# Another way to the global maximum, clips on GpSimd, and other orders at both ends of a Mamba kernel

## The reference

```
x, z = split(h @ W_in.T)                        # 256 channels each
x    = silu(conv4(x) + conv_b)                  # causal, per channel
dt, B, C = split(x @ Wx.T)                      # 64, 16, 16
dt   = softplus(dt @ Wdt.T + bdt)
s[t] = exp(dt*A) * s[t-1] + dt*x*B[t]           # 16 states per channel
y    = (sum_n s*C + x*D) * silu(z);   out = y @ W_out.T
x1   = layernorm(h + out_fwd + flip(out_rev))
xn   = layernorm(x1, eps 1e-3) * ln_gamma + ln_beta
beta = mean|w|;   w_q = clip(round(w / (beta + 1e-5)), -1, 1)
gamma = max|xn| over the whole tensor
q    = clip(xn * 128/gamma, -128 + 1e-5, 128 - 1e-5)
result = layernorm(x1 + (q @ w_q) * gamma*beta/128)
```

## Time and profile before

| | |
|---|---|
| three runs | 901.25, 902.7, 907.84 us; median 902.7 us |
| the profiled execution | 902.61 us, of which the span of the trace is 900.7 us |
| busy in the span | PE 644.8, DVE 790.4, ACT 698.7, POOL 808.6 us |
| mean granted clock of TensorE | 0.857 of full speed |
| DMA | 108.11 MB, mean 120 GB/s |

### The profile page before, as it was taken

How to read it: one execution, slowest core, us unless ns; L and a number is a source line. 1 busy time by engine, 2 the same in 40 slices (tenths; PEclk the granted TensorE clock), 3 DMA queues, 4 the chain that set the end, 5 groups by cost and what they waited for, 6 DMA issues and landing times. The chain is left out here.

```text
span 900.7 us, 9785 instructions
## 1 busy us (share of the span) xinstructions
PE 644.8 (72%) x2624; PEld 268.8 (30%) x2624; DVE 790.4 (88%) x807; ACT 698.7 (78%) x1214; POOL 808.6 (90%) x393
## 2 busy tenths in 40 slices
PE   7667786867777785958678685968569696557473
PEld 4323232313333231413233231423223132213223
DVE  2378999999898999999898999999898989999956
ACT  3587888886998888886997888887897888965514
POOL 0396999999999999999999999999999999999823
PEclk9769797979799797989899697989899798878787
DMA  3774647472675566473585556373584556484003
GB/s 64 184 172 93 147 90 144 103 156 72 122 185 104 117 139 136 96 158 80 118 189 101 113 128 134 102 156 97 106 178 85 129 111 132 112 163 164 24 1 94
DMA packets 79287, 108.11 MB, mean 120 GB/s; under 512 B 40832, under 2 KB 54144, under 8 KB 78976
## 3 DMA queue, kind: packets, MB, share of 16 engines
q1 hardware_dynamic: 79232, 107.48, 54.4%
HBM read 33.80 MB, written 6.55 MB: 45 GB/s over the span
## 5 line engine op out<-in xcount | busy, mean ns | idle before, releaser
L532 POOL TENSOR_TENSOR dbx<-step_rep,bc_rep 128x1024 f32<-128x1024 f32 x192 | 452.4, 2373 | 12.9 <-DMA step_rep<-step 10.8
L542 POOL TENSOR_TENSOR ch<-hs,bc_rep 128x1024 f32<-128x1024 f32 x128 | 303.1, 2368 | 21.5 <-PE y_ps L1295 19.4
L770 ACT ACTIVATE da_ps<-step_rep,neg_a 128x512 f32<-128x512 f32 x384 | 257.7, 697 | 79.1 <-DVE hs L1042 78.1
L1042 DVE TENSOR_TENSOR_SCAN hs<-da_ps,dbx 128x512 f32<-128x512 f32 x192 | 220.9, 1209 | 29.7 <-ACT da_ps L770 27.4
L1042 DVE TENSOR_TENSOR_SCAN hs<-da_ps,carry,dbx 128x512 f32<-128x512 f32 x192 | 232.9, 1268 | 15.5 <-ACT da_ps L770 12.8
L1295 PE MATMUL y_ps<-ch,stack 128*32 128x512 f32 x1024 | 158.0, 692 | 106.7 <-DVE ch L953 77.0
L698 ACT ACTIVATE dbx_tok<-c_ps,b_cols 128x256 f32<-128x256 f32 x256 | 152.9, 711 | 11.7 <-PE c_ps L1345 7.9
L953 DVE TENSOR_TENSOR ch<-hs,c_ps 128x2048 f32<-128x2048 f32 x60 | 135.9, 2266 | 0.0
L1243 PE MATMUL pre<-h_t,w_conv 128*128 128x512 f32 x248 | 117.1, 616 | 12.7 <-ACT xs L656 10.7
L1286 PE MATMUL c_ps<-x_dbl,select 128*128 128x512 f32 x136 | 98.2, 813 | 25.8 <-DVE ch L953 20.4
L1357 PE MATMUL da_ps<-ident,dbx_tok 128*128 128x128 f32 x512 | 75.6, 285 | 39.8 <-DVE hs L1042 39.6
(11 more groups left out here) (178 smaller groups left out, 621.6 us busy)
## 6 DMA issues: line engine op xcount, KB each, us to landing
step_rep<-step SPq DMA_DIRECT2D x128, 512.0 KB, 8.7
bc_rep<-bc_rows SPq DMA_DIRECT2D x48, 512.0 KB, 5.0
h_res<-in_L_attn_hidden_states SPq DMA_DIRECT2D x4, 512.0 KB, 8.1
x_rows<-xn SPq DMA_DIRECT2D x7, 256.0 KB, 7.8
h_in<-in_L_attn_hidden_states SPq DMA_DIRECT2D x3, 512.0 KB, 8.5
xn_rows<-xhat SPq DMA_DIRECT2D x6, 256.0 KB, 2.0
bc_rep<-x_rows SPq DMA_DIRECT2D x1, 1536.0 KB, 11.9
step_rep<-xn_rows SPq DMA_DIRECT2D x1, 1536.0 KB, 6.5
```

What stands on the lines that cost most here:

```text
L532: nc.gpsimd.tensor_tensor(dbx[:, n % RING], dtx_rep[:, r], b_rep[:, s % 2, k, :].unsqueeze(1).to_broadcast([P, 2, CHUNK]), ALU.mult).then_ ...
L542: nc.gpsimd.tensor_tensor(ch[:, n % RING], hs[:, n % RING], c_rep[:, s % 2, k, :].unsqueeze(1).to_broadcast([P, 2, CHUNK]), ALU.mult).then ...
L770: nc.scalar.activation(bank, dt_rep[:, r, e, :], ACT.Exp, scale=neg_a[:, half_of(unit), 2 * (unit % 2) + e, g, k:k + 1]).then_inc(da_ready, 1)
L1042: nc.vector.tensor_tensor_scan(in_scan_order(hs[:, n % RING, e, :], s), in_scan_order(factor, s), in_scan_order(term, s), initial, ALU.mul ...
```

## The change

Four things are changed, beside the names of semaphores (`first_dt` goes; `ones_ready`, `limits_ready` and `clipped_pool` come).

The global maximum: DVE writes the identity matrix times the column of the partitions' maxima (into `w_raw`, which is no longer used); PE multiplies a matrix of ones with it, so that each partition of the result holds all 128 maxima in its columns; DVE reduces them along the columns to gamma. POOL only writes the ones, into the first columns of `h_t`. The small products that follow are put in the order limits first, scales after. The product uses the bank of chunk 6, so chunk 6's residual start moves behind the wait for its clip.

The clips: DVE clips chunks 0 and 1; POOL clips 2, 3, 4, 5 ahead of its first power, and 7, 6 behind that power and ahead of the second.

The last sums: PE runs the residual product, then the last `add_units`, then the first half of the output product.

The first chain: ACT applies Silu straight from PSUM with the bias, half by half; PE transposes the weights ahead of the second half's convolution and makes x_dbl's first product as soon as the first half is there; ACT applies softplus straight from PSUM to each half of u. The counts in later waits are lowered by what the first group no longer signals; later groups keep their instructions.

The diff, without the list of semaphore names:

```diff
@@ -329,6 +329,14 @@
...
         LAST_ORDER = (0, 1, 2, 3, 4, 5, 7, 6)
+        VECTOR_CLIPS, POOL_CLIPS = (0, 1), ((2, 3, 4, 5), (7, 6))
+        ones, one_each = h_t[:, 0:P], w_raw[:]
+        gamma, inverse, scale_out, scale, limit, minus_limit = (tiny[:, k:k + 1] for k in range(5, 11))
+        def clip(eng, j):
+            t = slice(j * CHUNK, (j + 1) * CHUNK)
+            return eng.tensor_scalar(xn_t[:, t], xn_t[:, t], limit, minus_limit, ALU.min, ALU.max)
         LAST_PIECES = ((0, 1), (2, 3), (4, 5), (7,), (6,))
@@ -546,7 +554,7 @@
...
                 q = NG * b + s
-                pool.wait_ge(dt_ready, q + 1)
+                pool.wait_ge(dt_ready, q)
                 pool.wait_ge(xs_ready, q + 1)
@@ -589,7 +597,7 @@
...
             nc.gpsimd.partition_all_reduce(tiny[:, 1:2], tiny[:, 0:1], P, REDUCE.add).then_inc(w_sum_all, 1)
-            pool.wait_ge(dt_ready, 1)
+            pool.wait_ge(u_taken, 2)
             pool.wait_ge(xs_ready, 1)
@@ -608,9 +616,16 @@
...
-            pool.wait_ge(max_ready, 2 * BATCH + 1)
-            nc.gpsimd.partition_all_reduce(tiny[:, 5:6], tiny[:, 4:5], P, REDUCE.max).then_inc(all_max, 1)
+            nc.gpsimd.memset(ones, 1.0).then_inc(ones_ready, 1)
+            pool.wait_ge(limits_ready, 1)
+            pool.wait_ge(xn_in, 16)
+            for j in POOL_CLIPS[0]:
+                clip(nc.gpsimd, j).then_inc(clipped_pool, 1)
             for c in range(len(LAST_PIECES)):
+                if c == 1:
+                    for j in POOL_CLIPS[1]:
+                        clip(nc.gpsimd, j).then_inc(clipped_pool, 1)
                 pool.wait_ge(mv_last_ready, 2 * (c + 1))
@@ -655,7 +670,7 @@
...
                 if stage == "silu":
-                    act.wait_ge(conv_sb, DT * (q + 1))
+                    act.wait_ge(conv_sb, DT * (q + 1) - 1)
                     nc.scalar.activation(xs[:, par], xs[:, par], ACT.Silu).then_inc(xs_ready, 1)
@@ -669,10 +684,9 @@
...
                     act.wait_ge(u_ps, 2 * q + a + 1)
-                    if not zero and a == 0:
-                        act.wait_ge(dt_ready, q)
-                    bank = c_ps[:, 1, :] if zero and a else pre[:]
-                    nc.scalar.activation(u[:, a], bank, ACT.Identity, bias=bdt[:, g, a:a + 1]).then_inc(u_taken, 1)
+                    if q >= 2 and a == 0:
+                        act.wait_ge(dt_ready, q - 1)
+                    nc.scalar.activation(u[:, a], pre[:], ACT.Identity, bias=bdt[:, g, a:a + 1]).then_inc(u_taken, 1)
                 if stage == "softplus":
@@ -814,19 +828,19 @@
...
             act.wait_ge(conv_b_in, 16)
-            prepare(0, 0, "take conv0")
+            act.wait_ge(conv_ps, 1)
+            nc.scalar.activation(xs[:, 0, 0, :], pre[:], ACT.Silu, bias=conv_b[:, FWD, 0:1]).then_inc(conv_sb, 1)
             copy_ht(0, 1)
-            prepare(0, 0, "take conv1")
-            prepare(0, 0, "silu")
+            act.wait_ge(conv_ps, 2)
+            act.wait_ge(conv_sb, 1)
+            nc.scalar.activation(xs[:, 0, 1, :], c_ps[:, 0, :], ACT.Silu, bias=conv_b[:, FWD, 1:2]).then_inc(xs_ready, 1)
             nc.scalar.preload_act_table_set(SOFTPLUS)
...
             prepare(0, 0, "copy x_dbl")
-            prepare(0, 0, "take u0")
-            act.wait_ge(u_taken, 1)
-            nc.scalar.activation(step[:, 0, 0, :], u[:, 0], ACT.Softplus).then_inc(first_dt, 1)
-            prepare(0, 0, "take u1")
-            act.wait_ge(u_taken, 2)
-            nc.scalar.activation(step[:, 1, 0, :], u[:, 1], ACT.Softplus).then_inc(dt_ready, 1)
+            for a in range(DT):
+                act.wait_ge(u_ps, a + 1)
+                nc.scalar.activation(step[:, a, 0, :], c_ps[:, 1, :] if a else pre[:], ACT.Softplus,
+                                     bias=bdt[:, FWD, a:a + 1]).then_inc(u_taken, 1)
             nc.scalar.preload_act_table_set(EXP)
@@ -910,8 +924,8 @@
...
                 nc.vector.tensor_copy(wdt_t[:].rearrange("p g a m -> p (g a m)"), da_ps[:, 2, :]).then_inc(weights_sb, 1)
-                dve.wait_ge(first_dt, 1)
-                dve.wait_ge(xs_ready, 1)
+                dve.wait_ge(u_taken, 1)
+                dve.wait_ge(conv_sb, 1)
                 nc.vector.tensor_tensor(step[:, 0, 1, :], step[:, 0, 0, :], xs[:, 0, 0, :], ALU.mult).then_inc(first_dtx, 1)
@@ -1098,30 +1112,28 @@
...
-            gamma, inverse, scale_out, scale, limit, minus_limit = (tiny[:, k:k + 1] for k in range(5, 11))
             dve.wait_ge(max_ready, 2 * BATCH)
-            nc.vector.tensor_reduce(tiny[:, 4:5], part_max[:], X, ALU.max).then_inc(max_ready, 1)
-            def clip(c):
-                t = slice(c * CHUNK, (c + 1) * CHUNK)
-                nc.vector.tensor_scalar(xn_t[:, t], xn_t[:, t], limit, minus_limit, ALU.min, ALU.max).then_inc(clipped, 1)
+            chained(nc.vector.tensor_reduce(tiny[:, 4:5], part_max[:], X, ALU.max))
+            nc.vector.tensor_scalar(one_each, ident[:], tiny[:, 4:5], None, ALU.mult).then_inc(max_ready, 1)
             dve.wait_ge(all_max, 1)
+            chained(nc.vector.tensor_reduce(gamma, da_ps[:, 2, 0:P], X, ALU.max))
+            nc.vector.tensor_scalar(limit, gamma, (QB - QUANT_EPS) / QB, None, ALU.mult).then_inc(small_dve, 1)
+            nc.vector.tensor_scalar(minus_limit, gamma, -(QB - QUANT_EPS) / QB, None, ALU.mult).then_inc(limits_ready, 1)
             nc.vector.reciprocal(inverse, gamma).then_inc(small_dve, 1)
             nc.vector.tensor_scalar(scale_out, gamma, tiny[:, 2:3], 1.0 / QB, ALU.mult, ALU.mult).then_inc(small_dve, 1)
-            nc.vector.tensor_scalar(limit, gamma, (QB - QUANT_EPS) / QB, None, ALU.mult).then_inc(small_dve, 1)
             small[0] += 3
-            chained(nc.vector.tensor_scalar(minus_limit, gamma, -(QB - QUANT_EPS) / QB, None, ALU.mult))
+            dve.wait_ge(small_dve, small[0])
             nc.vector.scalar_tensor_tensor(scale, inverse, QB, scale_out, ALU.mult, ALU.mult).then_inc(small_dve, 1)
...
             dve.wait_ge(xn_in, 16)
-            clip(LAST_ORDER[0])
+            dve.wait_ge(limits_ready, 1)
+            clip(nc.vector, VECTOR_CLIPS[0]).then_inc(clipped, 1)
             dve.wait_ge(small_dve, small[0])
...
             nc.vector.tensor_scalar(w_q_scaled, w_q[:], scale, None, ALU.mult).then_inc(wq_scaled, 1)
-            for j in LAST_ORDER[1:]:
-                clip(j)
+            for j in VECTOR_CLIPS[1:]:
+                clip(nc.vector, j).then_inc(clipped, 1)
@@ -1235,7 +1247,7 @@
...
                 elif q:
-                    pe.wait_ge(conv_sb, DT * q + 1)
+                    pe.wait_ge(conv_sb, DT * q)
                 else:
@@ -1243,6 +1255,14 @@
...
                 ins.then_inc(conv_ps, 1)
+            def make_first_x_dbl():
+                pe.wait_ge(weights_sb, 1)
+                pe.wait_ge(conv_sb, 1)
+                nc.tensor.matmul(pre[:], wx_half(FWD, 0), xs[:, 0, 0, :], start=True, stop=False)
+                pe.wait_ge(xs_ready, 1)
+                nc.tensor.matmul(pre[:], wx_half(FWD, 1), xs[:, 0, 1, :], start=False, stop=True).then_inc(x_dbl_ps, 1)
@@ -1365,9 +1385,9 @@
...
                 elif h_e == 0:
-                    pe.wait_ge(conv_sb, DT * (NG * (b + 1) + 2))
+                    pe.wait_ge(conv_sb, DT * (NG * (b + 1) + 2) - 1)
                 else:
-                    pe.wait_ge(conv_sb, DT * (NG * (b + 1) + 3))
+                    pe.wait_ge(conv_sb, DT * (NG * (b + 1) + 3) - 1)
                 for t in range(TT):
@@ -1438,10 +1458,10 @@
...
             transpose_h(0, 1)
+            transpose_weights()
             convolve(0, 0, 1, None)
-            transpose_weights()
+            make_first_x_dbl()
             pe.wait_ge(select_ready, 3)
-            make_x_dbl(0, 0, (weights_sb, 1))
             pe.wait_ge(weights_sb, 2)
@@ -1456,9 +1476,6 @@
...
                 if a == 0:
-                    pe.wait_ge(h_res_ready, 16 * BATCH)
-                    pe.wait_ge(xn_sb, 2 * BATCH - 1)
-                    nc.tensor.matmul(pre[:], ident[:], h_res[:, 0:TT, :].rearrange("p t m -> p (t m)"), start=True, stop=False)
                     pe.wait_ge(g_half, 1)
@@ -1477,8 +1494,11 @@
...
+            pe.wait_ge(h_res_ready, 16 * BATCH)
+            pe.wait_ge(xn_sb, 2 * BATCH - 1)
+            nc.tensor.matmul(pre[:], ident[:], h_res[:, 0:TT, :].rearrange("p t m -> p (t m)"), start=True, stop=False)
+            add_units(BATCH - 1, NG - 1, UNITS - 2)
             last_output_half(0)
-            add_units(BATCH - 1, NG - 1, UNITS - 2)
             last_output_half(1)
@@ -1492,12 +1512,19 @@
...
             pe.wait_ge(x1_ready, TT * 2 * BATCH)
+            pe.wait_ge(ones_ready, 1)
+            pe.wait_ge(max_ready, 2 * BATCH + 1)
+            nc.tensor.matmul(da_ps[:, 2, 0:P], ones, one_each, start=True, stop=True).then_inc(all_max, 1)
             start_last(7)
-            start_last(6)
...
             for i, j in enumerate(LAST_ORDER):
-                pe.wait_ge(clipped, i + 1)
+                if j in VECTOR_CLIPS:
```

(13 more changed lines are left out.)

## The result

The changed kernel takes 897.9 us (median of 12 runs, 892.6 to 900.1) beside 903.4 us for the kernel before (12 runs): ratio 0.9932 [0.9913, 0.995]. A second set of runs of both kernels gave 897.7 beside 903.9 us, 0.9931 [0.9907, 0.9956]. Forecast were 896.9 us, a range of 894.2 to 900.4, and a change too small to tell from none by the measure of 1%; all three hold. The time alone would also fit rival (a), which had 898.0 us. What decides between the two is the tail.

A forecast was written before the change was run, and what follows sets the result against it. The prediction took GpSimd to bound the long middle, unchanged in length, with gains in tail and start: 902.6 − 5.2 (ACT's earlier start) − 0.5 (first chain) = 896.9 us, range 894.2 to 900.4.

The forecast's parts named there:

- rival (a): Tail clips: VectorE and GpSimd take turns, tail gain 4.05, total 898.0 us, or 899.4 at the lower clock; chance 0.28.
- Bound and middle: Long middle from 80 us: runs at GpSimd's pace, 40.00 of 40 us busy, and keeps its length.
- Sums first: Tail on PE: last sums run right after the residual product, bringing everything up to the maximum 0.95 us earlier.
- Maximum: Tail: gamma at 873.15 instead of 877.29, 4.1 us earlier, of which 3.2 from the missing all-reduce.
- GpSimd's clip: Tail: one clip on GpSimd taken as 0.8 us, between bounds of 0.29 and 1.27.
- rival (b): Tail: GpSimd's clips are dear; above about 1.3 us each GpSimd sets the tail, 905.1 us at 2.6; chance 0.07.
- What DVE's clips lose: Tail: DVE's clips beside GpSimd's lose one wait of 0.5 us, between 0 and 1.2.
- Clock: Output products: after a pause of about 1.1 us PE runs at 2.4 GHz, 1.95 us per two chunks.
- ACT's start: Tail: ACT starts at 881.6 instead of 886.79, 5.2 us earlier, then needs its 9.87 if fed.
- First chain: Start: x_dbl's copy ends at 20.0 against 20.51; 0.5 us reaches the middle, bounds 0 to 1.9.
- Rival (c): Start: first chain gains nothing because moved transposes delay the second convolution; 897.4 us, or 898; chance 0.10.
- Rival (d): Start: middle follows the softplus part, 1.9 instead of 0.5, and DVE does not wait at its clips; 895.0 us; chance 0.08.

The follow-up runs named there:

- e1: Changed kernel with the first chain as in the kernel before; ratio to the kernel before 0.9941 [0.9922, 0.9961], tail 32.06 us.
- e5: Changed kernel with the last sums behind the first half of the output product again; ratio to the kernel before 0.9947 [0.9933, 0.996], tail 31.09 us.
- e6: Changed kernel with GpSimd's first clip waiting until both DVE clips are done; ratio to the kernel before 0.9928 [0.9904, 0.9953], tail 29.88 us.
- e2: Kernel before with the changed first chain alone, tail as before; ratio to the kernel before 0.9986 [0.9965, 1.0006], tail 35.57 us.
- h1: Changed kernel with the last normalisation in eight one-chunk pieces instead of five; ratio to the kernel before 0.9924 [0.9898, 0.995], tail 30.29 us.
- h2: Changed kernel with GpSimd's clips waiting for DVE's two and chunk 7's last activations moved to DVE; ratio to the kernel before 0.9947, tail 29.01 us.
- e3: Changed kernel with GpSimd's all-reduce back for the maximum; ratio to the kernel before 1.0014 [0.9998, 1.003], tail 37.87 us.
- e7: Changed kernel with the all-reduce back and all eight clips on DVE; ratio to the kernel before 0.9993 [0.9978, 1.0007], tail 34.76 us.
- e8: Changed kernel with DVE clipping chunk 0 four times over beside GpSimd's four clips; one run, tail 34.51 us.

## Why the prediction was right, and where it was not

- *Bound and middle.* Right. The middle takes 818.2 to 821.7 us in the profiles with the old start (e1, before twice) and 818.0 to 821.7 in the eleven with the new one. The gain that the runs show is in the tail.
- *Sums first*, 0.95: e5 gives 0.90.
- *Maximum*, gamma 4.1 earlier with the sums: 3.90 (16.06 to 12.16). PE did wait for ACT's x1 rows last, as forecast. The product with ones and the reduction took 0.79 from its start to gamma where 0.71 stood.
- *GpSimd's clip*, 0.8 between bounds of 0.29 and 1.27: 0.755 alone, 0.84 as the mean of the four that run beside DVE's. A price from the middle of wide bounds came out near; rival (b), dear clips, is out.
- *What DVE's clips lose*, 0.5 as one wait: 0.31 (e6). "DVE's clips stretch" was one of the prediction's own signs of being wrong, and they did, from 0.54 to 0.85. The sum stood because the allowance of 0.5 covered it. Here luck helped: gamma came 0.24 later behind the residual product than forecast (12.16 for 11.92), the clips lost 0.2 less, and so the weight was ready at 13.76 for 13.77. Rival (a) had what seems to be the mechanism, turns, and the wrong price: each DVE instruction was to wait out a whole GpSimd clip. Instead the first is issued 0.2 behind GpSimd's start and ends 0.27 after its end, and the weight (0.28) isn't delayed by a clip at all. The row I weighed against it, the four-column add, was too small to show a turn.
- *Clock.* The 2.4 GHz level was taken as given. It held in seven of eight profiles with such a pause; where it didn't (e1) the tail lost 1.6. The forecast should have had it as a chance.
- *ACT's start* came 20.30 behind the residual product; 881.6 less 861.23 is 20.37. It was fed throughout.
- *First chain*, 0.5: 0.61 for the store, in the seven profiles of eleven in which the first convolution was short; in the other four the store came 1.2 to 1.7 later than with the old chain. That the store's gain reaches the middle, which the prediction took from b_cols standing behind it on SP's queue, no run shows: the transfers in between differ by more. Rival (c), nothing, is therefore not out; e2's 0.9986 [0.9965, 1.0006] can't tell 0.6 us from none. Rival (d), 1.9 in the middle's start, finds no support: counted from the convolution, the first profile of after begins its middle 1.0 later than before's, the second 0.3 earlier, and the earliest of all (h1) 0.9 earlier.
- *Where I read wrongly.* I wrote that ACT's end with the last store is the end. It is the third piece with a megabyte of stores (h2); the sum came out because all pieces moved alike. And I read the 7.04 us of idle time ahead of the first power as a wait for DVE alone. A second wait of some 6.6 us behind a pool configuration lay in it, which made the clips' move depend on the maximum's (e3 against e7). In this change both parts came together, so the sum wasn't touched.

## What to carry to other kernels

Ahead of a move to GpSimd, look for pool configurations on its queue on both sides of a library operation: here each was followed by about 6 us of nothing, and the one behind it hides easily under a wait for another engine. At the end of a kernel, ask which piece of work the last megabyte of stores waits for, not which instruction ends last. And measure a short chain from an event of its own engine: the start of the trace moved by over 1 us here, more than the change to the first chain was worth.

## What the runs showed of the hardware that was not expected

- The all-reduce, a library operation on GpSimd, costs twice: 5.6 us from the configuration to the all-reduce, and 6.6 us from the next configuration to the first ordinary instruction (e3).
- DVE's and GpSimd's clips over 512 columns hold each other up by less than a clip: where they meet, one of GpSimd takes 0.92 in place of 0.755 us and one of DVE 0.85 in place of 0.54 (e8, e6).
- The first convolution (eight products) took 3.67 us in ten profiles and 5.50 to 6.02 in four (e2, e7, e8, h2), behind the same work and the same pause of 0.83, while the granted clock read 1.00 throughout. In e2 the products between 9.43 and 12.85 begin 0.86 us apart, in the changed kernel's profile 0.43. In those four ACT's first product by tokens came 34.8 to 36.2 us behind the convolution's start, in the other ten 32.4 to 34.4. All four have the new first chain, of eleven profiles that have it, and none of the three with the old; nothing that PE does ahead of this convolution differs between the two. Whether the new chain brings it on or chance put all four there, and what makes it long, was not settled; if the chain does, it costs more in such an execution than it gains in the others.
